# Gate-weight parts and the first two rectifications on GpSimd, in a fused patch, graph, attention and expert kernel

## What is computed

```python
h = p @ W_embed + b_embed + sin_positional_encoding(N, HIDDEN)[None]
for i in range(3):
    hw = h @ W_gcn[i]
    agg = hw * snorm
    agg = agg.at[:, dst].add(hw[:, src] * enorm)
    h = jax.nn.relu(agg + b_gcn[i])
h = h @ W_out + b_out
...
h = jnp.concatenate([h, txt], axis=1)                 # 861 tokens
h = h + attention(_layernorm(h))                      # 4 heads of 16
h = h + experts(_layernorm(h))                        # shared MLP + 2 of 4 experts
# in experts:
gates = jax.nn.softmax(x @ gW + gb, axis=-1)
topv, topi = jax.lax.top_k(gates, TOPK)
topw = jax.nn.softmax(topv, axis=-1)
```

## Time and profile before

| | |
|---|---|
| median of 3 runs | 4932.01 us (4928.61 to 4933.14) |
| the profiled execution, whole | 4926.7 us |
| its span on the core | 4924.8 us |
| TensorE matmuls busy | 4716.8 us, 96% |
| VectorE busy | 3192.5 us, 65% |
| ScalarE busy | 3001.4 us, 61% |
| GpSimd busy | 1678.4 us, 34% |
| granted TensorE clock, mean | 0.984 |

### The profile page before, as it was taken

One profiled execution on the slowest core, in us unless ns is written; L12 is line 12 of the kernel. 1 busy time (PEld: TensorE's weight loads), 2 busy tenths in 40 slices (PEclk: granted clock), 3 DMA queues, 4 the chain that ended last, 5 costly groups with the idle time before them and its releaser, 6 DMA issues.

```text
span 4924.8 us, 80913 instructions
## 1 busy us (share of the span) xinstructions
PE 4716.8 (96%) x29262; PEld 3129.6 (64%) x29262; DVE 3192.5 (65%) x7342; ACT 3001.4 (61%) x6165; POOL 1678.4 (34%) x1678
## 2 busy tenths in 40 slices
PE   7599999999999999999999999999999999999997
PEld 5466666666666666666666666666666666666654
DVE  3366666666666667666667666667666667666663
ACT  2256666666666666666656666666666666656665
POOL 1224234333334333333333333333333333423322
PEclk9799999999999999999999999999999999999998
DMA  3432433433333333343332343333343343343220
GB/s 106 94 78 78 89 85 77 88 78 74 86 86 83 80 84 72 82 86 82 80 86 69 84 86 83 80 86 74 79 89 83 77 89 74 82 86 72 34 48 6
DMA packets 193397, 385.98 MB, mean 78 GB/s; under 512 B 74986, under 2 KB 118634, under 8 KB 193002
## 3 DMA queue, kind: packets, MB, share of 16 engines
q1 hardware_dynamic: 191978, 379.91, 34.1%
q10 hardware_dynamic: 1024, 0.89, 0.1%
HBM read 309.13 MB, written 109.26 MB: 85 GB/s over the span
## 4 chain that ended last, share of the span: by engine, by line
PE 75%; DVE 11%; ACT 7%; issue 2%; DMA 2%; POOL 1%; ACTq 0%; SPq 0%; DVEq 0%; another core or an unknown queue 0%; POOLq 0%
PE ps L1234 15%; PE ps L1224 13%; PE ps L1246 12%; PE ps L1278 9%; DVE neg_max_halves L1011 8%; PE ps L1296 6%; PE ps L1334 4%; ACT probs L896 4%; PE ps L1355 3%; PE ps L1269 3%; PE ps L367 2%; PE ps L1284 2%; PE ps L1323 2%; PE ps L1302 1%; DMA image_rows<-image_by_row 1%
## 5 line engine op out<-in xcount | busy, mean ns | idle before, releaser
L1011 DVE TENSOR_REDUCE neg_max_halves<-ps 123x1 f32<-123x432 f32 (+1 forms) x3584 | 2001.4, 599 | 764.1 <-PE ps L1246 748.7
L896 ACT ACTIVATE probs<-ps 123x432 f32<-123x432 f32 x3584 | 1691.3, 542 | 659.8 <-PE ps L1224 623.1
L1246 PE MATMUL ps<-k_stack,q_stack 96*123 96x432 f32 x3584 | 1291.6, 395 | 38.8 <-DMA k_stack<-qk_scratch 22.3
L1224 PE MATMUL ps<-q_stack,k_stack 97*123 97x432 f32 x3584 | 1252.3, 394 | 54.3 <-ACT probs L896 12.6
L1246 PEld LDWEIGHTS ps<-k_stack,q_stack 96*123 96x123 f32 x3584 | 637.4, 186 | 419.6 <-issue 273.2
L1224 PEld LDWEIGHTS ps<-q_stack,k_stack 97*123 97x123 f32 x3584 | 641.0, 185 | 340.8 <-issue 107.6
L1234 PE MATMUL ps<-probs,v_and_one 123*32 123x432 f32 x7168 | 760.8, 538 | 1.6 <-ACT probs L896 1.6
L959 ACT ACTIVATE hidden<-ps,plain_w 128x432 f32<-128x432 f32 x640 | 400.8, 634 | 148.5 <-PE ps L1296 148.5
L1278 PE MATMUL ps<-adjacency,parts_hi 112*128 112x392 f32 x1344 | 462.0, 344 | 3.3 <-DVE parts_lo L1033 3.2
L1278 PE MATMUL ps<-adjacency,parts_lo 112*128 112x392 f32 x1344 | 458.2, 341 | 0.0
L822 POOL TENSOR_TENSOR nodes_T<-nodes_T,dinv_row 128x392 f32<-128x392 f32 x128 | 131.0, 1024 | 847.3 <-ACT nodes_T L908 846.1
(11 more groups left out here) (158 smaller groups left out, 6232.7 us busy)
## 6 DMA issues: line engine op xcount, KB each, us to landing
image_rows<-image_by_row SPq DMA_DIRECT2D x256, 586.9 KB
q_stack<-qk_scratch SPq DMA_DIRECT2D x256, 216.0 KB, 7.8
k_stack<-qk_scratch SPq DMA_DIRECT2D x256, 216.0 KB, 9.0
image_by_row<-in_x SPq DMA_DIRECT2D x192, 196.0 KB
qk_scratch<-parts_hi SPq DMA_DIRECT2D x64, 432.0 KB, 2.9
qk_scratch<-parts_lo SPq DMA_DIRECT2D x64, 432.0 KB, 3.6
out<-tokens SPq DMA_DIRECT2D x64, 215.2 KB
tokens_next<-in_txt SPq DMA_DIRECT2D x64, 19.2 KB
```

The costliest lines, as they stand in the source:

```text
L896: act.activation(P[:, (g * 2 * NB + unit) % SLOTS, h, :], T[0:BLK, 0:HW], ACT.Exp, scale=SCALE).then_inc(free[r], 1)
L1011: v.tensor_reduce(NM[:, qb * HEADS + h, half:half + 1], T[0:BLK, 0:keys], AX.X, ALU.max, negate=True).then_inc(free[r], 1)
L1224: mm = pe.matmul(T[0:BLK, 0:cn], KS[:, g % 2, h, kb * BLK:(kb + 1) * BLK], QS[:, g % 2, h, c0:c0 + cn], start=True, stop=True)
L1246: mm = pe.matmul(T[0:BLK, 0:cn], QS[0:SHIFT_ROW, g % 2, h, qb * BLK:(qb + 1) * BLK], KS[0:SHIFT_ROW, g % 2, h, c0:c0 + cn], start=True, st ...
```

## The change

The first part of the change moves the rectification of layers 0 and 1 from ScalarE to GpSimd. GpSimd's step now waits for VectorE's instruction, runs one TENSOR_SCALAR (add the bias, maximum with 0) in place, waits for it, and multiplies by `dinv` as before. ScalarE keeps layer 2. The second part moves the five instructions that make the bfloat16 parts of the gate weights from VectorE to GpSimd, in the same places of the list, and lets VectorE's next gate weights wait until the parts of the image before have been made.

```diff
                     elif kind == "relu" and st[2] < 2:
                         c = slice(st[3] * GHALF, (st[3] + 1) * GHALF)
-                        counted(pool, ht_relu, nth, st)
+                        emptied(pool, turn, ("gagg", *st[1:]))
+                        settle(pool.tensor_scalar(HT[:, c], HT[:, c], w("b_gcn", st[2], 1), 0.0, ALU.add, ALU.max))
                         pool.tensor_tensor(HT[:, c], HT[:, c], dinv[:, c], ALU.mult).then_inc(ht_scaled, 1)
...
+                    elif kind == "part0":
+                        counted(pool, g_weight, nth, ("gweight", st[1]))
+                        filled(pool, turn, ("wt", st[1] - 1))
+                        done(pool.tensor_copy(GP[:, :, 0, :], GW[:, :, :]), st)
+                    elif kind in ("rest0", "rest1"):
+                        part = int(kind[-1])
+                        need(("part%d" % part, st[1]))
+                        done(pool.tensor_tensor(GR[:, part, :, :], GR[:, 0, :, :] if part else GW[:, :, :],
+                                                GP[:, :, part, :], ALU.subtract), st)
+                    elif kind == "part1":
+                        need(("rest0", st[1]))
+                        done(pool.tensor_copy(GP[:, :, 1, :], GR[:, 0, :, :]), st)
+                    elif kind == "part2":
+                        need(("rest1", st[1]))
+                        pool.tensor_copy(GP[:, :, 2, :], GR[:, 1, :, :]).then_inc(g_parts, 1)
...
-                    elif kind == "relu":
+                    elif kind == "relu" and st[2] == 2:
...
                         elif kind == "gweight":
                             need(("grec2", g))
                             counted(v, hb_ready, hb_no, ("hb", g - 1, 2 * EXPERTS))
+                            counted(v, g_parts, nth, ("part2", g - 1))
...
-                        elif kind == "part0":
-                            counted(v, g_weight, nth, ("gweight", g))
...
-                            v.tensor_copy(GP[:, :, 2, :], GR[:, 1, :, :]).then_inc(g_parts, 1)
...
-                                counted(pe, ht_relu, nth, ("relu", p, 2, 1))
+                                counted(pe, ht_relu, relu_no, ("relu", p, 2, 1))
```

More of the change, by code:

```diff
@@ L1166, in run @@
                             counted(v, hb_ready, hb_no, ("hb", g - 1, 2 * EXPERTS))
+                            counted(v, g_parts, nth, ("part2", g - 1))
                             v.tensor_tensor(GW[:, :, :], GZ[:, 1, :, :], inverse.unsqueeze(2).to_broadcast(sh),
                                             ALU.mult).then_inc(g_weight, 1)
-                        elif kind == "part0":
-                            counted(v, g_weight, nth, ("gweight", g))
-                            filled(v, turn, ("wt", g - 1))
-                            done(v.tensor_copy(GP[:, :, 0, :], GW[:, :, :]), st)
-                        elif kind == "rest0":
-                            need(("part0", g))
-                            done(v.tensor_tensor(GR[:, 0, :, :], GW[:, :, :], GP[:, :, 0, :], ALU.subtract), st)
-                        elif kind == "part1":
-                            need(("rest0", g))
-                            done(v.tensor_copy(GP[:, :, 1, :], GR[:, 0, :, :]), st)
-                        elif kind == "rest1":
-                            need(("part1", g))
-                            done(v.tensor_tensor(GR[:, 1, :, :], GR[:, 0, :, :], GP[:, :, 1, :], ALU.subtract), st)
-                        elif kind == "part2":
-                            need(("rest1", g))
-                            v.tensor_copy(GP[:, :, 2, :], GR[:, 1, :, :]).then_inc(g_parts, 1)
                     elif kind == "wb":
@@ L1206, in run @@
                 turn, nth = turns(steps), ordinal(steps)
+                relu_no = ranks(steps, lambda st: st[0] == "relu" and st[2] == 2)
                 scaled_no = ranks(steps, lambda st: st[0] == "relu" and st[2] < 2)
```

## The result

The changed kernel takes **5031.15 us** (5024.95 to 5040.56), the kernel before, beside it on the same chip, 4929.16 us. The ratio is **1.0207 (1.0193 to 1.0221)**: slower by 102 us. The prediction was 4930 us with a range of 4918 to 4957, so it was wrong, and by more than its range allowed.

The account below looks back on a forecast made before the run. TensorE was taken to set the pace, losing time in small waits. Terms of +7.5 (layer 1), +1.3 (pair 0) and -10.9 (odd images' gates) gave -2.1 us, so 4930 us was expected against a median of 4932.0, range 4918 to 4957.

Parts of the forecast that it names:

- Where the loss would arise: Layer 1's GpSimd queue: four instructions in series delay TensorE by 0.26 us a pair, +7.5 us over 29 pairs.
- The rival "slower": Layer 1's GpSimd chain with D near the two-input product: 4955 us at D = 1.02; chance 0.25.
- The duration D: Time of GpSimd's new TENSOR_SCALAR: taken as 0.60 us, bounds 0.49 and 1.02; wrong if over 0.8.
- 60D - 38: Whole predicted change in us as a function of D; passes +10 at D = 0.80 and +23 at 1.02.
- The gate parts, odd images: Moving them off VectorE frees TensorE's waits for maxima: 0.35 us a pair, -10.9 us over 31 pairs.
- both waits gone: Sign in the odd image's gates: TensorE's waits of 0.40 and 0.30 us for the maxima disappear.
- The gate parts, even images: Made inside GpSimd's `hb` chain, at 0.2 to 0.3 us each: hidden before `wt` with 3 us to spare, 0 gained.
- Pair 0: Program start: two rectifications queue behind GpSimd's packing of patches, 2D + 2 x 0.07 = +1.3 us, once.
- Layer 0: Its rectification on GpSimd makes a shorter chain, but TensorE does not wait for it: 0.
- ScalarE's relief: 128 instructions of 0.62 us leave ScalarE, but nothing is queued behind them: 0.

Follow-up runs that it names:

- The two filled kernels: Kernel before with 7 unread matmuls at two idle spells near the value projection (4918.36 us); changed kernel with those plus 12 ahead of layer 2 (4985.48 us).
- parts_filled: Kernel before with only the gate parts moved to GpSimd, plus 7 unread matmuls at two idle spells near the value projection; 4905.26 us, ratio 0.9946.
- parts_only: Kernel before with only the gate parts moved to GpSimd, rectification left on ScalarE; 4925.91 us, ratio 0.9998.
- layer0_parts_row_dma: Kernel before with gate parts and layer 0's rectification on GpSimd, and the row maxima's transfer issued by SyncE instead of ScalarE; 4891.6 us, ratio 0.9933.
- last_half_on_act: Kernel before with rectification of layer 0 and layer 1's first half on GpSimd, layer 1's second half on ScalarE, gate parts on VectorE; 4947.06 us, ratio 1.0033.
- filled_pause: Changed kernel plus 12 idle matmuls on TensorE in the pause ahead of layer 2; 5009.27 us, ratio 1.0168.
- change_all_filled: Changed kernel plus 12 idle matmuls ahead of layer 2 and 7 at the idle spells around the even image's value projection; 4985.48 us, ratio 1.0114.
- parts_row_dma_by_sync: Kernel before with only the gate parts on GpSimd, and the row maxima's transfer issued by SyncE instead of ScalarE; 4890.59 us, ratio 0.9917.
- before_filled: Kernel before plus 7 unread matmuls at two idle spells near the value projection; 4918.36 us, ratio 0.9977.

## Why the prediction was wrong, step by step

- **Where the loss would arise: right.** Layer 1's POOL queue, four instructions in series, was the place named; the two products end 0.1 us before the formula puts them with the measured D. The rival "slower" described this mechanism.
- **The duration D: the step that failed.** "The nearest rows" for a TENSOR_SCALAR were the CAST (0.49 scaled) and the two-input product (1.02), and the prediction took the product as an upper bound. D is 1.60, twice the 0.8 above which the prediction called itself wrong. Nothing in the trace made either row a bound: they are other operations on the same engine, and it was only plausible that one tensor input must be cheaper than two. With the measured D the prediction's formula, 60D - 38, gives +58 us, and 4990. The two filled kernels, with the clock held at its upper level, differ by 148.28 - 146.40 = 1.88 us a pair; the formula's terms give 2 x 1.60 - 0.94 - 0.35 = 1.91. The term was mis-sized: the prediction had 0.26 us a pair, and with the measured D it is 2.26.
- The Trainium skill's "GPSIMD Engine Reference", section "Performance versus the Vector engine", has about 1.03 cycles per element for up to two operations, which gave an estimate of 0.52 us. The measurement decides against it: 1.19 us for one operation and 1.53 for two.
- **The clock: a step that was missing.** The prediction counted a wait as long as it lasts. A pause of 2.15 us is followed in most pairs by a stretch at half the clock, which costs 1.4 us or more: some 35 of the 102 us by the runs, a third of the loss. The prediction's sum has no term for it. It also made a small idle spell that the prediction did not look at into the place that takes gains back.
- **The gate parts, odd images: right in size, but paid out only where the clock lets it.** 0.35 us a pair was counted. The eight steps of the earlier trace rows took 2.05 us; in parts_filled they take 1.66, which is 0.39:

```profile
1416.06 0.36 PE L1250 MATMUL ps<-k_stack,q_stack 96*123 96x432 f32 x1
...
1417.72 1.05 PE L1338 MATMUL ps<-hidden,plain_w 128*64 128x492 f32 x4
```

  It came from the wait of 0.40 us in the earlier trace rows alone. The other, 0.30 us ahead of line 1334, is still there with the maxima long done (PEld of parts_filled, below), so VectorE was not its cause, and the prediction's sign "both waits gone" held for one only. In time the term gave 0 in parts_only and 13 us in parts_filled, with 10.9 predicted.

```profile
1417.72 0.20 PEld L1338 LDWEIGHTS ps<-hidden,plain_w 128*64 128x64 f32 x4 [0.30 <-issue]
```

- **The gate parts, even images: right.** They take 0.21 to 0.25 us each; the last one ends at 2597.22, and `wt` starts 3.7 us later, where 3 us to spare were predicted:

```profile
2597.01 0.21 POOL L861 CAST gate_weight_parts<-gate_weight_rest 123x28 bf16<-123x28 f32 x1
...
2600.91 0.55 PE L1341 MATMUL ps<-ident_bf,gate_weight_parts 123*12 123x123 bf16 x7
```

- **Pair 0:** the formula 2D + 0.14 gives 3.3 us with the measured D, and the first `gw` starts 3.4 us later (115.53 against 112.11).
- **Layer 0 and ScalarE: nearly right.** Layer 0 was put at 0 and costs 0.09 us a pair. The reason given, that the new chain is shorter, fails with the measured D: GpSimd takes 1.60 us where ScalarE took 0.62. TensorE comes to its part late enough to hide nearly all of that. ScalarE's relief was put at 0, and none is seen: layer0_parts_row_dma spares ScalarE half of the moved rectifications and has pairs 0.1 us longer.
- **The sum of it:** 30 pairs of 1.88 us and 3.4 at the start are 60, and the clock adds 35: 95, against 102 measured. The missing 7 lie between these 60 and the 67 by which the two filled kernels differ. In their traces a long fall in pair 20 (4.7 us) and the longer pair 2 (1.1) are part of it; the rest I have not placed.

## What to carry to other kernels

An operation that the trace does not show has no upper bound in other operations of the same engine; where a chain on the critical path holds it several times, ask from which duration the sign turns (here 0.63 us, in the formula), and treat everything above as open. A pause of TensorE can cost twice, as time lost and as work at the lower clock behind it: here one of 2.15 us did in most pairs, and one of 0.47 us at the same place never. Look for the idle spells behind which the clock already falls: here they swallowed a real gain of 13 us whole, and filling them gave the kernel before 11 us, removing one of them 30. To price the clock's part of a change, fill both kernels, before and after, and compare these. When a gain that the trace of a pair shows is missing from the time, compare pair by pair before giving up the theory.

## What the runs showed of the hardware

- GpSimd's TENSOR_SCALAR on 128x392 fp32 takes 1.19 us (one operation, constant), 1.26 (one, column), 1.53 (two, constants), 1.60 (two, one column), the same to 0.01 us each time, while its TENSOR_TENSOR of that size takes 1.02 and its CAST of 448 elements 0.56.
- In the changed kernel 21 falls of TensorE's clock in pairs 1 to 30 lie at the pause ahead of layer 2 (2.15 us, in the last pair 2.74). In last_half_on_act none lies behind one of 0.47 us at the same place. But falls lie behind the spells of 0.52 and 0.35 us at the value projection: 5 before, 14 in parts_only, 19 in filled_pause, with the same spells in all three. What decides in which pair they bring a fall was not settled.
- Some falls have no idle spell ahead of them at all: pair 20 of change_all_filled, pair 18 of parts_row_dma_by_sync and pairs 7 and 8 of layer0_parts_row_dma have one of 10.2 us each, with no idle time of TensorE over 0.15 us in the 5 us before, and take 4.7 us longer. Their cause is open.
- Matmuls whose result nobody reads kept the clock up and cost nothing that shows: an undisturbed pair takes 146.4 us in before_filled as in before.
